# The heads-of-16 run: an order for each engine, z transposed and output weights whole in plain fp32, the norm's constant on Pool

## The chip, the cores and the metric

The kernel runs on one core of one Trainium2 chip. The metric is the device time of one execution in microseconds (us). Before the change it was 1670.71 us, the median of 3 runs (1670.12 to 1672.01). The engines are TensorE (PE in the profile, with its weight loads apart as PEld), VectorE (DVE), ScalarE (ACT), GpSimd (POOL) and SyncE (SP), which issues the DMAs.

## The reference

Two decoder layers with a norm after each part, on x of 16 sequences x 128 positions x 256 features. The six parts, each as x = norm(x + part(x)):

1. causal self-attention with 16 heads of 64
2. eight dense experts with relu (256 to 512 and back), weighted by gates that are gathered from the context
3. a gated FFN with 2 shared and 16 routed experts, top 2
4. self-attention with 16 heads of 16, only keys within 8 positions
5. cross-attention with 16 heads of 16, keys and values from ctx (16 x 128 x 128), with biases
6. eight experts with gelu (256 to 512 and back), all summed, scaled by a gate

Parts 4 and 5 are the heads-of-16 run. For part 4 the reference computes

```python
qkv = (x @ Wqkv).reshape(b, n, 3, H, HD)
attn = where(band, q @ k.T * HD ** -0.5, -1e9); attn = softmax(attn)
out = (attn @ v).transpose(0, 2, 1, 3).reshape(b, n, c) @ Wproj + bproj
x = (r - mean(r)) / sqrt(var(r) + 1e-5)      # r = x + out
```

Part 5 is the same with q from x, k and v from the context, and a bias on each.

## The kernel before, in words

**Precision.** Most products are split: an operand is held as a high part of type fp32r and a low part, the rest of it (fp32r too), and `split3` (L81 to L85) multiplies high x high, high x low and low x high into one sum. To split a tile costs two instructions: ACT writes the high part out of PSUM, DVE subtracts it from PSUM's value to get the low part. Products of plain fp32 tiles also occur (P times V, transposes by the identity); a plain fp32 product shows as two records in the trace, a transpose as one.

**Tiling of the run.** The 16 sequences go in groups of 4; the four groups of part 4 and then the four of part 5 make 8 groups G. A sequence has 16 heads in 4 quads of 4 heads, so there are 128 quads n and 32 sequences B. Step n of the run stands for quad n in all engines' programs. Per quad:

- "s": PE computes the scores of 4 heads, 128 x 512, into one of two PSUM banks (L1576 adds the band mask, L1579 the products); DVE takes the negated row maximum (L1803); ACT takes four exponentials (L1705).
- "t": PE transposes the four P tiles (L1589); DVE (even quads, L1808) or ACT (odd, L1679) copies them out.
- "pv": PE multiplies with V (L1603), the four heads in four column strips, the row sums in a 17th column.

Per sequence:

- "ze": ACT empties the bank of P-V products (L1722), the next sequence's first P-V product waits for that.
- "zb": PE transposes back (L1617). "zn" (DVE): reciprocal (L1765) and product (L1767) give z.
- "zt": PE transposes z (L1625); ACT writes its high part `nzT_h` (L1726); DVE its low part `nzT_l` (L1813).
- "o": PE's output product, 2 x split3 = 6 products of 256 columns (L83 to L85 with `nzT`), with the output weights in halves.
- "na": DVE adds the residual (L1774). "ns": DVE takes statistics (L1779, L1780) and adds the epsilon (L1781), POOL raises to the power -0.5 (L1509). "nb": DVE writes the new X (L1786).

Fills "x", "k", "q", "v" prepare the next group: transposes of X and its split, projections to K, Q and V; x two fills of 4 transposes, k and q two each, v four. They and "zb" share two PSUM banks in turn. SP then lays keys and queries out, split in halves and by head, by 24 DMAs of 128 KB a group (L1433).

**What sets the order.** Semaphores alone hold the engines together; each engine works off a list in program order. `n_order` writes the list for PE, ACT and POOL; a step n holds s(n), t(n-2), pv(n-3), then per sequence ze at lag 6 (B = (n-6)/4), zb 7, zt 8, o 9, na 9, ns 10, nb 11, then a fill of the next group and, at the end of the run, work of the next stage: "mx" (transposes of X) and "mu" (the first up products of part 6). On ACT, t of an odd quad comes ahead of s. `n_order_vector` writes DVE's list: s(n), what was put off from the step before (zn of lag 7, zt of lag 8, a fill), t(n-2), na and ns of lag 10, nb of lag 12. So an engine that meets an item whose semaphore is not there yet stands, and all behind it stands too. POOL also splits weights (`beside`): those of part 5 at quad 0, two units of part 6 at quad 16, both at once.

## Time and profile before

| | |
|---|---|
| median of 3 runs | 1670.71 us |
| the profiled execution | 1671.6 us |
| its span, first to last instruction | 1669.8 us |
| PE busy | 1544.2 us, 92% |
| PE weight loads busy | 1331.2 us, 80% |
| DVE busy | 1010.4 us, 61% |
| ACT busy | 693.9 us, 42% |
| POOL busy | 180.0 us, 11% |
| mean granted TensorE clock | 0.982 of 2.4 GHz |

The prediction is made against the profiled execution. A row of the grouped views gives an engine's instructions of one kind, how often, their busy time and mean, and the engine's idle time just before them with what ended it. A matmul's end is modelled and includes the pipeline's latency: consecutive matmuls overlap in the rows, and what one takes up of the array is the distance of the starts.

### The profile page before, as it was taken

The page shows a single profiled execution, that of the slowest core. Times are in us where ns is not written, and L with a number is a line of the kernel's source. Part 1 is how long each engine was busy: PE and PEld are TensorE (multiplying, and loading weights), DVE is VectorE, ACT ScalarE, POOL GpSimd, SP SyncE. Part 2 cuts the span into 40 slices and gives each one's busy share as a digit, 9 for nine tenths or more (in the row PEclk, how much of TensorE's full clock was granted, in tenths as well). Part 3 has the DMA queues.
Part 4 walks back from the last instruction along what each step waited for, and adds up shares of the span by engine and source line. Part 5 has one row for each costly group of instructions (what it writes and reads, how often), then busy time and mean ns, then how long its engine had stood idle before and what let it go on. Part 6 is the DMA issues. An engine that isn't in the chain of part 4 may idle for free.

```text
span 1669.8 us, 28828 instructions
## 1 busy us (share of the span) xinstructions
PE 1544.2 (92%) x11176; PEld 1331.2 (80%) x11176; DVE 1010.4 (61%) x2177; ACT 693.9 (42%) x1809; POOL 180.0 (11%) x174
## 2 busy tenths in 40 slices
PE   6999999899999999899999788887778899999997
PEld 5888888689899989888888566666557798989896
DVE  6777677755545445766656666677774554444446
ACT  1444444522222222123333566677773344444443
POOL 1222222310000000020000330111110000000001
PEclk9999999999999999989999999999997899999999
DMA  6000100011101101000001965667640000000001
GB/s 203 2 14 1 39 2 1 26 37 38 31 32 37 38 17 45 19 20 14 32 0 19 128 77 72 78 85 113 80 65 14 13 26 26 26 25 13 25 13 50
DMA packets 43067, 66.52 MB, mean 40 GB/s; under 512 B 4561, under 2 KB 33489, under 8 KB 42833
## 3 DMA queue, kind: packets, MB, share of 16 engines
q1 hardware_dynamic: 42960, 65.09, 19.8%
q8 instruction: 69, 1.13, 0.3%
q14 instruction: 38, 0.30, 0.1%
HBM read 36.24 MB, written 2.10 MB: 23 GB/s over the span
## 4 chain that ended last, share of the span: by engine, by line
PE 78%; DVE 15%; issue 2%; ACT 2%; DMA 1%; SPq 1%; POOL 0%; DVEq 0%; POOLq 0%; ACTq 0%
PE ps L83 22%; PE ps L84 21%; PE ps L85 21%; DVE negm L1803 4%; PE ps L366 2%; PE ps L390 2%; PE ps L377 2%; PE ps L1579 1%; DVE nPT L1808 1%; PE ps L360 1%; DVE nz L1767 1%; DVE X L901 1%; PE ps L1576 1%; PE ps L1603 1%; DVE nzT_l L1813 1%
## 5 line engine op out<-in xcount | busy, mean ns | idle before, releaser
L863 DVE TENSOR_TENSOR m6hT_l<-m6h,m6hT_h 128x512 fp32r<-128x512 f32 x128 | 88.5, 692 | 189.9 <-ACT m6hT_h L768 189.7
L770 ACT ACTIVATE m2hT_h<-ps 128x512 fp32r<-128x512 f32 x128 | 76.4, 597 | 285.9 <-PE ps L85 285.9
L865 DVE SCALAR_TENSOR_TENSOR m2hT_l<-ps,m2hT_h 128x512 fp32r<-128x512 f32 x128 | 88.5, 691 | 160.5 <-ACT m2hT_h L770 160.4
L767 ACT ACTIVATE m6h<-ps,m6b 128x512 f32<-128x512 f32 x128 | 88.0, 688 | 222.5 <-PE ps L85 207.9
L1705 ACT ACTIVATE nPr<-ps,negm 128x128 f32<-128x128 f32 x512 | 145.2, 371 | 72.0 <-DVE negm L1803 71.2
L83 PE MATMUL ps<-w_h,m6hT_h 128*128 128x256 f32 x512 | 145.9, 285 | 2.4 <-DVE X L901 1.8
L85 PE MATMUL ps<-w_h,m6hT_l 128*128 128x256 f32 x512 | 146.3, 286 | 0.0
L84 PE MATMUL ps<-w_l,m6hT_h 128*128 128x256 f32 x512 | 145.8, 285 | 0.0
L1803 DVE TENSOR_REDUCE negm<-ps 128x4 f32<-128x512 f32 x128 | 87.9, 688 | 89.0 <-PE ps L1579 88.3
L85 PE MATMUL ps<-m2w_h,m2hT_l 128*128 128x256 f32 x448 | 126.8, 283 | 0.0
L84 PE MATMUL ps<-m2w_l,m2hT_h 128*128 128x256 f32 x448 | 126.7, 283 | 0.0
L83 PE MATMUL ps<-m2w_h,m2hT_h 128*128 128x256 f32 x448 | 126.3, 282 | 0.0
L83 PE MATMUL ps<-m6XT_h,w_h 128*128 128x512 f32 x256 | 103.4, 404 | 9.0 <-DVE m6hT_l L863 9.0
L83 PEld LDWEIGHTS ps<-w_h,m6hT_h 128*128 128x128 f32 x512 | 98.7, 193 | 8.6 <-issue 2.4
L84 PE MATMUL ps<-m6XT_l,w_h 128*128 128x512 f32 x256 | 102.9, 402 | 0.0
L84 PEld LDWEIGHTS ps<-w_l,m6hT_h 128*128 128x128 f32 x512 | 98.7, 193 | 5.2
L85 PE MATMUL ps<-m6XT_h,w_l 128*128 128x512 f32 x256 | 102.1, 399 | 0.0
L85 PEld LDWEIGHTS ps<-w_h,m6hT_l 128*128 128x128 f32 x512 | 98.4, 192 | 0.0
L445 ACT ACTIVATE wPr<-ps,negm 128x128 f32<-128x128 f32 x256 | 90.8, 383 | 4.8 <-DVE negm L513 4.8
L83 PEld LDWEIGHTS ps<-m2w_h,m2hT_h 128*128 128x128 f32 x448 | 85.6, 191 | 4.7
L83 PE MATMUL ps<-m2XT_h,m2w_h 128*128 128x512 f32 x224 | 88.9, 397 | 0.3 <-DVE m2hT_l L865 0.2
L84 PEld LDWEIGHTS ps<-m2w_l,m2hT_h 128*128 128x128 f32 x448 | 85.6, 191 | 4.0
(288 smaller groups left out, 4274.6 us busy)
## 6 DMA issues: line engine op xcount, KB each, us to landing
nKm<-nKc_h SPq DMA_DIRECT2D x64, 128.0 KB, 4.6
nQs<-nQc_h SPq DMA_DIRECT2D x64, 128.0 KB, 6.0
raw<-in_w_e1i SPq DMA_DIRECT2D x9, 512.0 KB, 3.3
raw<-in_w_e1o SPq DMA_DIRECT2D x9, 512.0 KB, 3.3
raw<-in_w_e6i SPq DMA_DIRECT2D x9, 512.0 KB, 3.4
raw<-in_w_e6o SPq DMA_DIRECT2D x9, 512.0 KB, 3.4
raw<-in_w_a SPq DMA_DIRECT2D x8, 512.0 KB, 4.5
nKm<-nKc_l SPq DMA_DIRECT2D x32, 128.0 KB, 5.4
```

What stands on the lines that cost most here:

```text
L83: nc.tensor.matmul(out, wh, xh, start=start, stop=False, **kw)
L84: nc.tensor.matmul(out, wh, xl, start=False, stop=False, **kw)
L85: return nc.tensor.matmul(out, wl, xh, start=False, stop=stop, **kw)
L366: last = nc.tensor.matmul(ps[:, WSB[half], i * S:(i + 1) * S], W.QT[G % 2][rows64, 4 * u + i, tok], W.KT[G % 2][rows64, 4 * u + i, tok], s ...
L377: last = nc.tensor.transpose(ps[:, WTB[half], i * S:(i + 1) * S], W.Pr[:, p % 3, half, i, :], ident[:, :])
L445: last = nc.scalar.activation(W.Pr[:, p % 3, half, j, :], ps[:, WSB[half], j * S:(j + 1) * S], ACT.Exp, bias=negm[:, n % 4, j:j + 1], accu ...
L767: nc.scalar.activation(c.h32[:, u % 2, :], ps[:, u % 2, :], ACT.Gelu, bias=bias)
L770: nc.scalar.activation(c.hT[0][:, ch, :], ps[:, u % 2, :], ACT.Relu).then_inc(c.s["hi_ready"], 1)
L863: last = nc.vector.tensor_tensor(c.hT[1][:, ch, :], c.h32[:, u % 2, :], c.hT[0][:, ch, :].bitcast(F32), ALU.subtract)
L865: last = nc.vector.scalar_tensor_tensor(c.hT[1][:, ch, :], ps[:, u % 2, :], 0.0, c.hT[0][:, ch, :].bitcast(F32), ALU.max, ALU.subtract)
L1705: last = nc.scalar.activation(N.Pr[:, i % 4, j, :], ps[:, SB[i % 2], j * S:(j + 1) * S], ACT.Exp, bias=negm[:, i % 4, j:j + 1])
L1803: nc.vector.reduce_max(negm[:, i % 4, :], ps[:, SB[i % 2], :].rearrange("p (h k) -> p h k", h=QH), AX.X, negate=True).then_inc(s["s_max"], 1)
```

## The change

- Each engine gets an order of its own: `n_order` for PE, `n_order_scalar`, `n_order_vector`, `n_order_pool`. Lags before and after: PE zb 7 and 7, zt 8 and 9 (now between the scores and the P transposes), o 9 and 10; ACT ze 6 and 5, zt 8 and 8, with the copy of P of an odd quad ahead of the exponentials in both; DVE zn 8 in effect and 8, na 10 and 11, ns 10 and 14, nb 12 and 16; POOL's power 10 and 14, with the residual (na) at 11.
- Fills stand at steps 0, 2, 4, 5, 6, 8, 9, 10, 12, 14 of a group, not at 0, 1, 4 to 11. "mx" 4 and 5 stand at 13 and 14, not 11 and 12. The run has 17 steps after the last quad, not 12.
- z transposed is one plain fp32 tile `nzT` in two buffers, written by ACT alone; the low half and DVE's subtraction go. The output weights are also kept whole in fp32 (`wo4`, `wo5`, in the room of their low halves), and the output product is 2 plain fp32 products of 256 columns, not 6 split ones.
- `split_unit` writes the whole copy with `tensor_copy`, in place of the subtraction.
- The addition of the norm's epsilon moves from DVE to POOL, which then waits for itself before the power.
- POOL's splits are single units at quads 3, 7, 19 and 23.

```diff
-    A5.wq, A5.wk, A5.wv, A5.wo = view(wA5, 0, DC, D), view(wA5, 512, 1, D), view(wA5, 768, 1, D), view(wA5, 1024, DC, D)
+
+    wo4 = Region(nc, r3.start + (2048 + 1536) * 4, 2 * KB).place("wo4", [P, DC * D], F32)
+    wo5 = Region(nc, r1.start + (1536 + 1024) * 4, 2 * KB).place("wo5", [P, DC * D], F32)
+    A4.wo, A5.wo = (w[:, :].rearrange("p (k n) -> p k n", k=DC) for w in (wo4, wo5))
+    A5.wq, A5.wk, A5.wv = view(wA5, 0, DC, D), view(wA5, 512, 1, D), view(wA5, 768, 1, D)
...
-    def split_unit(v, base, k, w, ncols, on=nc.vector, quarter=None):
+    def split_unit(v, base, k, w, ncols, on=nc.vector, quarter=None, whole=None):
+
...
         on.tensor_scalar(w[0], raw[k % 2][:, 0:ncols], 1.0, None, ALU.mult).then_inc(split_hi, 1)
         v.wait_ge(split_hi, base + (k + 1))
+        if whole is not None:
+            n_whole = whole.shape[1]
+            last = on.tensor_copy(whole, raw[k % 2][:, ncols - n_whole:ncols])
+            if n_whole < ncols:
+                last.then_inc(split_whole, 1)
+                on.tensor_tensor(w[1][:, 0:ncols - n_whole], raw[k % 2][:, 0:ncols - n_whole], w[0][:, 0:ncols - n_whole].bitcast(F32),
+                                 ALU.subtract).then_inc(split_whole, 1)
+                v.wait_ge(split_whole, 2)
+                v.sem_inc(prep_done, 1)
+            else:
+                last.then_inc(prep_done, 1)
+            return
         on.tensor_tensor(w[1], raw[k % 2][:, 0:ncols], w[0].bitcast(F32), ALU.subtract).then_inc(prep_done, 1)
...
-    N.zT = pair(m, "nzT", [P, DC, S])
+    N.zT = m.place("nzT", [P, 2, DC, S], F32)
...
-    M_X_AT = (6, 7, 8, 9, 11, 12)
+    M_X_AT = (6, 7, 8, 9, 13, 14)
...
-        return [("x", (G, 0)), ("x", (G, 1)), None, None, ("k", (G, 0)), ("k", (G, 1)), ("q", (G, 0)), ("q", (G, 1)),
-                ("v", (G, 0)), ("v", (G, 1)), ("v", (G, 2)), ("v", (G, 3))]
+        at = {0: ("x", 0), 2: ("x", 1), 4: ("k", 0), 5: ("k", 1), 6: ("q", 0), 8: ("q", 1),
+              9: ("v", 0), 10: ("v", 1), 12: ("v", 2), 14: ("v", 3)}
+        return {k: (kind, (G, j)) for k, (kind, j) in at.items()}
+    def n_fill_of(n):
+        G, k = divmod(n, NQ)
+        return [n_fills(G + 1)[k]] if G + 1 < NGG and k in n_fills(G + 1) else []
+    def n_quad(kind, n, lag=0):
+        return [(kind, n - lag)] if 0 <= n - lag < NQUADS else []
+    def n_seq(kind, n, lag):
+        return [(kind, (n - lag) // 4)] if (n - lag) % 4 == 0 and 0 <= (n - lag) // 4 < NSEQS else []
+    N_STEPS = NQUADS + 17
     def n_order():
-        order = [f for f in n_fills(0) if f]
-        for n in range(NQUADS + 12):
-            G, k = divmod(n, NQ)
-            step = [("s", n), ("t", n - 2), ("pv", n - 3)]
-            step += [(kind, (n - at) // 4) for kind, at in (("ze", 6), ("zb", 7), ("zt", 8), ("o", 9), ("na", 9), ("ns", 10), ("nb", 11))
-                     if (n - at) % 4 == 0]
-            of = {"s": NQUADS, "t": NQUADS, "pv": NQUADS}
-            order += [(kind, i) for kind, i in step if 0 <= i < of.get(kind, NSEQS)]
-            if G + 1 < NGG and k < 12 and n_fills(G + 1)[k]:
-                order.append(n_fills(G + 1)[k])
-            order += n_following(n)
+        order = list(n_fills(0).values())
+        for n in range(N_STEPS):
+            order += n_quad("s", n) + n_seq("zt", n, 9) + n_quad("t", n, 2) + n_quad("pv", n, 3)
+            order += n_seq("zb", n, 7) + n_seq("o", n, 10) + n_fill_of(n) + n_following(n)
+        return order
+    def n_order_scalar():
+        order = list(n_fills(0).values())
+        for n in range(N_STEPS):
+            order += n_quad("t", n, 2) + n_quad("s", n) + n_seq("ze", n, 5) + n_seq("zt", n, 8) + n_fill_of(n) + n_following(n)
+        return order
+    def n_order_vector():
+        order = list(n_fills(0).values())
+        for n in range(N_STEPS):
+            order += n_quad("s", n) + n_seq("zn", n, 8) + n_quad("t", n, 2)
+            order += n_seq("nb", n, 16) + n_seq("ns", n, 14) + n_seq("na", n, 11)
+            order += n_fill_of(n - 1) + n_following(n - 1)
+        return order
+    def n_order_pool():
+        order = []
+        for n in range(N_STEPS):
+            order += n_quad("s", n) + n_seq("na", n, 11) + n_seq("ns", n, 14)
         return order
     def n_following(n):
-    def n_order_vector():
-        order = [f for f in n_fills(0) if f]
-        late = []
-        for n in range(NQUADS + 13):
-            G, k = divmod(n, NQ)
-            steps = [("s", n)] if n < NQUADS else []
-            steps += late
-            if 0 <= n - 2 < NQUADS:
-                steps.append(("t", n - 2))
-            steps += [(kind, (n - at) // 4) for kind, at in (("na", 10), ("ns", 10), ("nb", 12))
-                      if (n - at) % 4 == 0 and 0 <= (n - at) // 4 < NSEQS]
-            late = [(kind, (n - at) // 4) for kind, at in (("zn", 7), ("zt", 8))
-                    if (n - at) % 4 == 0 and 0 <= (n - at) // 4 < NSEQS]
-            if G + 1 < NGG and k < 12 and n_fills(G + 1)[k]:
-                late.append(n_fills(G + 1)[k])
-            late += n_following(n)
-            order += steps
-        return order
...
-        for kind, i in n_order():
+        for kind, i in n_order_pool():
             if kind == "ns":
                 b = i % GB
                 pool.wait_ge(s["ln_var"], i + 1)
+                nc.gpsimd.tensor_scalar(veps[:, b:b + 1], mv[:, b, 1:2], LN_EPS, None, ALU.add).then_inc(s["eps_added"], 1)
+                pool.wait_ge(s["eps_added"], i + 1)
                 nc.gpsimd.tensor_tensor(rstd[:, b:b + 1], veps[:, b:b + 1], mhalf[:, b:b + 1],
                                         ALU.pow).then_inc(s["rstd_ready"], 1)
             elif kind == "na" and i % GB == GB - 1 and i + 1 < NSEQS:
                 residual(i // GB + 1)
+            elif kind == "s" and i in beside:
+                beside[i]()
             elif kind == "s" and i % NQ == 0:
                 G = i // NQ
-                if G in beside:
-                    beside[G]()
                 if NG - 1 <= G < NGG - 1:
                     context(G - NG + 1)
 
...
-                last = split3(nc, ps[:, EB, D:2 * D], N.zT[0][:, ch, :], N.zT[1][:, ch, :],
-                              c.wo[0][:, ch, :], c.wo[1][:, ch, :], ch == 0, ch == DC - 1)
+                last = nc.tensor.matmul(ps[:, EB, D:2 * D], N.zT[:, B % 2, ch, :], c.wo[:, ch, :],
+                                        start=ch == 0, stop=ch == DC - 1)
...
-        for kind, i in n_order():
+        for kind, i in n_order_scalar():
...
-                if i >= NQUADS - 2 and i % 2:
+                if i % 2:
                     transposed_p(i)
             elif kind == "s":
-                if i >= 2 and i % 2:
-                    transposed_p(i - 2)
                 act.wait_ge(s["s_max"], i + 1)
...
-                nc.scalar.activation(N.zT[0][:, :, :].rearrange("p a b -> p (a b)"), ps[:, EB, 0:D],
-                                     ACT.Identity).then_inc(s["zt_hi"], 1)
+                nc.scalar.activation(N.zT[:, i % 2, :, :].rearrange("p a b -> p (a b)"), ps[:, EB, 0:D],
+                                     ACT.Identity).then_inc(s["zt_ready"], 1)
...
-            link(nc.vector.bn_aggr(mv[:, b, :], stats[:, b, :]))
-            nc.vector.tensor_scalar(veps[:, b:b + 1], mv[:, b, 1:2], LN_EPS, None, ALU.add).then_inc(s["ln_var"], 1)
+            nc.vector.bn_aggr(mv[:, b, :], stats[:, b, :]).then_inc(s["ln_var"], 1)
...
-            elif kind == "zt":
-                v.wait_ge(s["zt_hi"], i + 1)
-                nc.vector.tensor_tensor(N.zT[1][:, :, :].rearrange("p a b -> p (a b)"), ps[:, EB, 0:D],
-                                        N.zT[0][:, :, :].rearrange("p a b -> p (a b)").bitcast(F32),
-                                        ALU.subtract).then_inc(s["zt_ready"], 1)
...
-            def split_a5():
-                for k in range(2):
-                    split_unit(pool, U_A5, k, cut(wA5, k * 768, 768), 768, nc.gpsimd, quarter=(2 * D, 3) if k == 0 else None)
-            def split_e6():
-                for k in range(2):
-                    split_unit(pool, U_E6, k, cut(slots6[0], k * RAW, RAW), RAW, nc.gpsimd)
-            n_pool(pool, {0: split_a5, 1: split_e6})
+            def split_a5(k):
+                split_unit(pool, U_A5, k, cut(wA5, k * 768, 768), 768, nc.gpsimd, quarter=(2 * D, 3) if k == 0 else None,
+                           whole=None if k == 0 else wo5[:, :])
+            def split_e6(k):
+                split_unit(pool, U_E6, k, cut(slots6[0], k * RAW, RAW), RAW, nc.gpsimd)
+            n_pool(pool, {3: lambda: split_a5(0), 7: lambda: split_a5(1), 19: lambda: split_e6(0), 23: lambda: split_e6(1)})
             mix_pool(pool, M6)
 
```

## Rows read from the trace of the kernel before

**Rows 1.** The page's busy table: engine, busy us, share of span, instructions.
```profile
PE 1544.2 (92%) x11176; PEld 1331.2 (80%) x11176; DVE 1010.4 (61%) x2177; ACT 693.9 (42%) x1809; POOL 180.0 (11%) x174
```

**Rows 2.** The row maxima by line: count, shortest/median/longest ns, first and last start.
```profile
L1803 DVE TENSOR_REDUCE negm<-ps x128: 680/691/693, 928.1 to 1255.2; 128x4 f32<-128x512 f32 x128
```

**Rows 3.** Windows: stretch, length, busy PE, PEld, DVE, ACT, POOL, clock, DMA, GB/s.
```profile
967.30:1012.00 44.70, 38.36 (x346) 28.79 (x345) 29.60 (x67) 29.07 (x87) 13.97 (x9) 1.00 0.58 72
...
1099.10:1139.40 40.30, 32.28 (x313) 24.35 (x312) 29.73 (x67) 29.61 (x88) 6.36 (x8) 1.00 0.65 87
...
1220.00:1255.20 35.20, 27.38 (x286) 20.14 (x288) 27.61 (x62) 27.79 (x85) 3.96 (x4) 1.00 0.46 69
```

**Rows 4.** Waits, 928 to 1268 us: us in total, times, longest.
```profile
ACT nPr L1705 <- DVE negm L1803: 71.2, 77, 11.9
...
PE ps L1625 <- DVE nz L1767: 19.6, 31, 0.9
...
PE ps L83 <- DVE nzT_l L1813: 13.2, 30, 0.7
PE ps L1603 <- issue: 9.2, 14, 0.8
...
PE ps L1603 <- ACT nzr L1722: 5.5, 7, 0.8
```

**Rows 5.** Waits of PE's weight loads, 928 to 1268 us.
```profile
PEld ps L1625 <- DVE nz L1767: 28.8, 32, 1.3
PEld ps L83 <- DVE nzT_l L1813: 21.6, 30, 1.0
...
PEld ps L1617 <- issue: 6.5, 31, 0.2
```

**Rows 6.** Lines by form, 960 to 1260 us: count, busy, mean ns, idle before.
```profile
L1576 PE MATMUL ps<-band,identb 128*128 128x512 bf16 x51 | 19.7, 387 | 0.0
...
L1509 POOL TENSOR_TENSOR rstd<-veps,mhalf 128x1 f32<-128x1 f32 x29 | 16.0, 550 | 190.2 <-DVE veps L1781 190.2
...
L1813 DVE TENSOR_TENSOR nzT_l<-ps,nzT_h 128x256 fp32r<-128x256 f32 x30 | 12.5, 415 | 0.0
```

**Rows 7.** Timeline, 1060 to 1082 us: start, length, instruction, merged count.
```profile
1059.82 0.41 PE L1603 MATMUL ps<-nPT,nV 128*17 128x128 f32 x8
...
1060.42 1.14 ACT L1705 ACTIVATE nPr<-ps,negm 128x128 f32<-128x128 f32 x4
...
1060.79 0.28 PE L84 MATMUL ps<-wA_l,nzT_h 128*128 128x256 f32 x1
...
1061.27 0.28 PE L85 MATMUL ps<-wA_h,nzT_l 128*128 128x256 f32 x1
```

**Rows 8.** Plain fp32 products of part 1 (by tile, then timeline) and bf16.
```profile
L390 PE MATMUL ps<-wPT,wV x416: 272/273/324, 62.9 to 299.6; 128*64 128x128 f32 x139
...
150.22 1.09 PE L390 MATMUL ps<-wPT,wV 128*64 128x128 f32 x16
...
151.25 0.60 PE L360 MATMUL ps<-causal,identb 128*128 128x512 bf16 x2
```

**Rows 9.** SP's issue of a layout DMA; the page's issues with landing.
```profile
1166.00 0.61 SPq L1433 DMA_DIRECT2D nQs<-nQc_h  x1
...
nQs<-nQc_h SPq DMA_DIRECT2D x64, 128.0 KB, 6.0
```

**Rows 10.** Timeline, the run's last sequence.
```profile
1267.13 0.38 ACT L1726 ACTIVATE nzT_h<-ps 128x256 fp32r<-128x256 f32 x1
...
1268.44 1.23 DVE L640 TENSOR_TENSOR w_l<-raw,w_h 128x1024 fp32r<-128x1024 f32 x1
...
1270.38 0.58 PE L83 MATMUL ps<-wA_h,nzT_h 128*128 128x256 f32 x1 [3.29 <-DVE nzT_l L1813]
```

**Rows 11.** Windows at the same place.
```profile
1265.40:1268.80 3.40, 0.81 (x4) 0.20 (x2) 2.82 (x6) 1.65 (x3) 0.39 (x1) 1.00 0.00 0
1268.80:1272.20 3.40, 1.82 (x8) 1.82 (x9) 1.66 (x4) 0.00 (x0) 0.00 (x0) 0.50 0.38 105
```

More of the change, by code:

```diff
@@ L170, in program @@
     split_hi = sem("split_hi")
+    split_whole = sem("split_whole")
     raw_loaded = [sem("raw_loaded0"), sem("raw_loaded1")]
@@ L195, in program @@
     A4.wq, A4.wk, A4.wv = ([t[:, :, i * D:(i + 1) * D] for t in qkv4] for i in range(3))
-    A4.wo = view(wA4, 1536, DC, D)
-    A5.wq, A5.wk, A5.wv, A5.wo = view(wA5, 0, DC, D), view(wA5, 512, 1, D), view(wA5, 768, 1, D), view(wA5, 1024, DC, D)
+    wo4 = Region(nc, r3.start + (2048 + 1536) * 4, 2 * KB).place("wo4", [P, DC * D], F32)
+    wo5 = Region(nc, r1.start + (1536 + 1024) * 4, 2 * KB).place("wo5", [P, DC * D], F32)
+    A4.wo, A5.wo = (w[:, :].rearrange("p (k n) -> p k n", k=DC) for w in (wo4, wo5))
+    A5.wq, A5.wk, A5.wv = view(wA5, 0, DC, D), view(wA5, 512, 1, D), view(wA5, 768, 1, D)
     A4.mask, A4.cross, A4.bq, A4.bk, A4.bv, A4.bo = band, False, None, None, None, row_bo4
@@ L1296, in steps @@
                         n, at = (768, k * 768) if k < 2 else (256, 1536 + (k - 2) * 256)
-                        split_unit(v, U_A4, k, cut(wA4, at, n), n, quarter=(D, k + 1) if k < 2 else None)
+                        split_unit(v, U_A4, k, cut(wA4, at, n), n, quarter=(D, k + 1) if k < 2 else None, whole=None if k < 2 else wo4[:, (k - 2) * D:(k - 1) * D])
                 elif kind == "c":
@@ L1349, in program @@
     N.s = signals("n", "g_full g_evac xt_hi qk_hi ct_hi ct_ready ctx_loaded s_full s_max p_ready pt_full pt_even pt_odd z_full "
-                       "z_zeroed zr_ready zb_full rec_done z_ready zt_full zt_hi zt_ready o_full r_done xb_ready ln_var rstd_ready x_done")
+                       "z_zeroed zr_ready zb_full rec_done z_ready zt_full zt_ready eps_added o_full r_done xb_ready ln_var rstd_ready x_done")
     N.q_laid = [sem(f"n_q_laid{j}") for j in range(2)]
```

## Prediction, before the changed kernel ran

> **What bounds the kernel now.** I read the page's busy table first [rows 1]: TensorE (PE) is busy 92% of the span. A share over all stages says little here, since the edit touches one stage, the heads-of-16 run, whose row maxima run from 928.1 to 1255.2 us, 128 of them, one per quad of heads [rows 2]. So I listed where those maxima start and cut the stage there, at every 16th, which is a group of 4 sequences [rows 3]. A group takes 44.7 us in the banded attention, 40.3 us in the cross attention, and 35.2 us at the end, where no projections of a next group lie in between. PE is busy 38.4, 32.3 and 27.4 us of these; VectorE (DVE) 29.6, 29.7, 27.6; ScalarE (ACT) 29.1, 29.6, 27.8. The granted clock is 1.00 (2.4 GHz). No engine is full: PE leads, and stands still at fixed places once per sequence.
>
> The waits name these places. PE's matmuls wait 19.6 us in 31 waits for z (the transposes of z, L1625), 13.2 us in 30 waits for the low half of z transposed (the output product's first, L83), and 9.2 + 5.5 us in 14 + 7 waits ahead of the P-V products (L1603), whose bank ACT has still to empty [rows 4]. The matmul rows understate it, because a matmul's modelled end reaches past the time in which it takes up the array. PE's weight loads show the hole itself: 28.8 us in 32 waits and 21.6 us in 30, against 0.21 us (6.5 in 31) that even a wait released in time leaves [rows 5].
>
> **Part by part, per sequence (32 of them).**
>
> 1. z's transposes go from the step that follows the division (lags 8 and 7 quads in PE's and DVE's order) to lag 9, behind that step's scores. The hole of 0.90 us shrinks to the usual 0.21: 0.69.
> 2. The output product goes from lag 9 to 10 and no longer waits for DVE. Today PE transposes z, ACT writes the high half (0.38 us [rows 10]), DVE, in its next step behind the maximum, the low half (0.415) [rows 6], and PE stands before it. Now ACT alone writes zT and PE has more than a step of other work. 0.72 less 0.21: 0.51.
> 3. The evacuation of z (kind "ze") moves up on ACT from lag 6 to 5, so it lies ahead of the exponentials of step 4B+6, and the P-V products at step 4B+7 find their bank free: 14.7/32 = 0.46.
> 4. Against it: the product itself. The split products start 0.12 us apart (four intervals from 1060.79 to 1061.27 [rows 7]): 0.72 for the six. Two plain fp32 products replace them. The trace has no plain fp32 product of 256 columns. It has 128-column ones [rows 8]: each is two records; 16 records in two concurrent column halves take 1.09 us, the last of them 0.27, so 0.82 for 7 intervals, 0.77 without the slow first (0.324 against 0.273): 0.11 for a pass over 128 columns. Two bf16 products of 512 columns take 0.60 together, the last of them 0.39 [rows 6, 8], so 0.21 to 0.22 for 512 columns: the plain pass is twice as slow per column. That product loads 64 columns of weights; L1603 with 17 loaded columns starts its second round after about the same 0.13 (0.41 less 0.28 [rows 7]), so it is not the load. At that rate: 2 products x 2 passes x 2 x 0.11 = 0.88 us, 0.16 more than today. The lower bound, if 0.11 were the time of any pass however long: 4 x 0.11 = 0.44, or 0.28 less than today. I take 0.88: the nearest row is the same kind of product; with the cheap end the sum below would be 14 us lower.
>
> The Trainium skill (FP8 and Floating Point Precision, section TensorE Precision Notes) says that true FP32 makes four passes through the array. By it two products of 256 columns would take 4 × 256 / 2.4 × 2 = 0.85 us, an estimate; it speaks against this edit as a saving on PE and sides with my dearer end.
>
> Sum per sequence: 0.69 + 0.51 + 0.46 − 0.16 = 1.50 us closable, 48.0 us for 32.
>
> 5. How much of it comes through? With all of it a cross-attention sequence would take 10.07 − 1.50 = 8.6 us. ACT needs 29.6/4 = 7.4 of that, its work unchanged in amount: 86%. DVE loses the low half (0.415) [rows 6] and a 128x1 addition: under 7.0, or 81%. 86% is just the share that PE holds in the banded groups today (38.4 of 44.7), the highest of any engine in this stage. So the full sum lies at the edge; and ACT now waits in its order for two things that PE issues a step later. I take two thirds, 1.0 us, and 32.0 us for the stage. Bounds: one third (16 us) and the whole with the cheap product (62 us).
> 6. DVE's relief and the spread of its work over the four steps of a sequence are not on the path: it is busy 29.7 of 40.3 us. Worth nothing by itself; without it, item 5 would be tighter.
> 7. Pool gets the epsilon add: a 128x1 operation beside a power of 0.55 us on the same shape [rows 6], between 0.1 and 0.6 us plus a semaphore round. DVE's "nb" asks for it 2 quads (over 4 us) after "ns"; Pool stands idle 190 us in this stretch before those powers. Nothing. If that cover went it would cost 0.6 per sequence on DVE, not on PE. Behind it on Pool stand the residual of the next group and the context split, both asked for more than a step later.
> 8. Weight preparation: the output weights keep their high pass and get a copy in place of the subtraction (two DVE units, equal instruction count), and Pool issues one instruction more, of 512 columns, at the start of the stage for weights used in its second half. Splitting the next stage's weights as two single units at steps 19 and 23 instead of both at 16 leaves Pool's powers less blocked; none of the large waits [rows 4] is for Pool, so nothing.
> 9. The fills stand further apart, q's second at step 8 instead of 7. SP lays out the queries behind it: 6 issues of 0.61 us and 6.0 us to landing [rows 9], some 10 us, with 7 steps (over 15 us) to go. SP's second half (12 issues and a landing, 13.3 us) must be there by step 8, 17 us at the new pace. The last two transposes of X for the next stage move from steps 11 and 12 to 13 and 14, behind the norm that they need (step 12 for sequence 27). Nothing.
> 10. The drain. For the last sequence PE stands 3.29 us before the output product, since DVE's low half waits behind the split of the next stage's weights, whose second instruction alone takes 1.23 us [rows 10]. ACT's copy of zT ends at 1267.51; with nothing of DVE between, the product could start by 1267.8 instead of 1270.38: 2.5 us. What follows on the chain to the last X (statistics, Pool, norm) gets up to 0.6 longer by Pool's add and lies beside the first down products and one up product. In the same stretch the granted clock falls to 0.50 (1.2 GHz) after PE had been busy 0.81 of 3.4 us, and PE works 1.82 of the next 3.4 us at it [rows 11], and, busy throughout, 3.4 us more; without the fall these 5.2 us would take 2.6 less. Between 0 and 2.6; I take 0, since nothing says that the fall would not then come at the next gap.
>
> Sum: 32.0 + 2.5 = 34.5 us. The profiled execution took 1671.6 us (span 1669.8 and 1.8 around it): 1637.1. It stands 0.9 above the median 1670.71, so against the median 1636.
>
> **Rivals.**
>
> A, all holes close: items 1 to 4 in full, the drain and the clock: 48.0 + 2.5 + 2.6 = 53.1, 1618 us. For it: ACT waits 71.2 us for the maximum alone [rows 4], more than it would have to give. Against: 86% on ACT in order.
>
> B, ACT or DVE become the bound early: a third of the holes comes through, 16 + 2.5 less, 1652 us. For it: the group without projections, where PE has 7.8 us of slack, still takes 35.2 us with three engines at 27.4 to 27.8. So more than PE's holes paces it.
>
> C, slower: ACT's new places. "ze" at lag 5 stands ahead of the next exponentials and waits for P-V products that PE issues in its next step, behind that step's scores and P transposes and behind whatever projection the step before had; "zt" at lag 8 likewise. A projection of six 512-column products is 6 × 0.22 = 1.3 us, four P transposes and the P-V products at 0.11 a pass some 0.6 more: up to 1.9 us of standing at each, 3.8 per sequence. ACT has 10.07 − 7.4 = 2.7 us to spare. From there on it costs: 1.1 us in each of the 28 sequences beside projections, +31 us, 1702 us. It speaks against it that the exponentials ahead of "ze" last 1.14 us [rows 7] and the P copy comes on top, which covers nearly all of a step without a projection, and that two score banks let PE run ahead.
>
> D, no change: an unseen loop of scores, maximum, exponentials sets the step. The loop is about 0.5 + 0.69 + 1.14 and latencies, 2.5 us for two quads, 1.25 per quad, while a quad takes 2.2 to 2.8. Hardly.
>
> **Chances.** Forecast (1625 to 1646) 0.55; A (below 1625) 0.17; B (1646 to 1667) 0.15; within 0.2% (3.3 us, what a measurement of this kernel can tell) 0.04; C 0.09. So faster 0.87, same 0.04, slower 0.09. The range 1616 to 1660 leaves out part of B and all of C.
>
> **What would show it.** In the changed profile: groups near 40 and 36 us instead of 44.7 and 40.3; PE's weight loads ahead of z's transposes and of the output product with holes near 0.2; the "nzr" wait gone; plain products of zT as four records per sequence, about 0.22 us apart (0.11 would be rival A's cheap end); ACT's share above 80% in a group, and its waits for the scores' maximum halved from 71 us. New ACT waits of over 1 us before its copies of z or zT, or PE waiting for exponentials, would be B or C. Pool's adds under 0.6 us, nobody waiting. I am wrong if groups stay above 42 and 39 us.

## The result, and the profile after

The changed kernel takes 1615.92 us (median of 4 runs, 1614.77 to 1618.39) against 1671.03 us for the kernel before (median of 4 here): ratio 0.9672, 95% interval 0.9655 to 0.9689, 55 us faster. I had forecast 1636. The direction was right and the mechanism mostly so; the size was not: the time lies on the lowest edge of the range of 1616 to 1660, where rival A (all holes close, 1618) stood with a chance of 0.17.

The stage first. These are windows of the changed kernel, cut like [rows 3] at the first row maximum of a banded group, of a cross group, and of the last one (stretch, length, busy PE, PEld, DVE, ACT, POOL, clock, DMA share, GB/s):

```profile
965.90:1003.90 38.00, 38.00 (x339) 29.04 (x338) 30.09 (x59) 28.40 (x88) 15.90 (x13) 1.00 0.63 84
1076.70:1108.60 31.90, 31.90 (x305) 24.54 (x303) 27.63 (x58) 28.35 (x87) 7.40 (x12) 1.00 0.81 109
1172.40:1206.80 34.40, 28.90 (x273) 21.03 (x272) 24.83 (x52) 27.09 (x83) 5.47 (x9) 0.95 0.47 76
```

The banded group fell from 44.7 to 38.0 us, the cross group from 40.3 to 31.9, and in both PE's busy time fills the stretch: no hole is left that its modelled ends would show. The last group did not follow (35.2 to 34.4, and its window covers 15 quads, as that of before does); PE stands in it for 5.5 us, and its granted clock was 0.95, not 1.00, which is 1.7 us at full rate. Starts of the row maxima give the sum: the first seven groups took 291.9 us and take 241.0, 50.9 less; from the start of the last group to the end of the span 449.8 and 444.2, 5.6 less; the run starts 3.3 us later in this execution (931.4 against 928.1 us), which differs from execution to execution: f3 and e4 below, with the same code up to there, start at 927.4 and 928.6. Together 53.2, the difference of the spans (1669.8 and 1616.6).

The waits of the changed kernel over 928 to 1215 us (total, times, longest) answer to [rows 4, 5]:

```profile
DVE negm L1828 <- PE ps L1607: 44.7, 78, 1.5
ACT nPr L1731 <- DVE negm L1828: 23.3, 32, 12.3
...
ACT nzT L1752 <- PE ps L1653: 18.3, 22, 2.8
...
PEld ps L1645 <- issue: 6.5, 31, 0.2
PEld ps L1662 <- issue: 6.5, 31, 0.2
PE ps L707 <- DVE m6XT_l L866: 5.0, 4, 2.2
...
PEld ps L1653 <- DVE nz L1793: 1.1, 3, 0.4
```

PE's hole before the transposes of z is 1.1 us in all (2.4 with the run's last sequence, at 1220) where it was 28.8; the output product's weights (L1662) start after the plain 0.21. ACT now waits 18.3 us for the transposes of z, the wait that rival C feared; in the full groups it costs nothing, since PE has no hole there. ACT's waits for the maximum fell from 71.2 us to 23.3 (one wait of 11.9 and of 12.3 us in each). Of the forms in 960 to 1210 us (count, busy us, mean ns, idle before) four answer to parts of the sum:

```profile
L1731 ACT ACTIVATE nPr<-ps,negm 128x128 f32<-128x128 f32 x460 | 131.9, 383 | 9.7 <-DVE negm L1828 9.7
...
L1662 PE MATMUL ps<-wo,nzT 128*128 128x256 f32 x116 | 32.8, 405 | 0.0
...
L1811 DVE TENSOR_SCALAR X<-nr,mv,rstd 128x256 f32<-128x256 f32 x29 | 14.2, 489 | 0.0
...
L1535 POOL TENSOR_SCALAR veps<-mv 128x1 f32<-128x1 f32 x29 | 6.3, 218 | 199.3 <-DVE mv L1806 199.3
```

And one output product in the timeline, four records merged, which take 1.13 us with the last one's 0.379 in it; behind it the run's last:

```profile
1176.11 1.13 PE L1662 MATMUL ps<-wo,nzT 128*128 128x256 f32 x4
...
1220.65 1.13 PE L1662 MATMUL ps<-wo,nzT 128*128 128x256 f32 x4 [0.47 <-ACT nzT L1752]
```

1.13 − 0.38 = 0.75 for three intervals, the first of them longer by 0.1 for the start after a wait: 0.216 a pass.

### The profile page after: what moved, and what is told of

It is laid out like the page before. It is cut to its first block, busy times and chain, and to the rows that moved or that the text cites. A ratio compares the mean times of both kernels' runs of the same rounds, so it can differ in the third digit from the quotient of the medians.

```text
span 1616.6 us, 28670 instructions
## 1 busy us (share of the span) xinstructions
PE 1541.5 (95%) x11112; PEld 1330.8 (82%) x11112; DVE 998.3 (62%) x2113; ACT 687.4 (43%) x1809; POOL 187.6 (12%) x207
## 3 DMA queue, kind: packets, MB, share of 16 engines
q8 instruction: 69, 1.13, 0.3%
## 4 chain that ended last, share of the span: by engine, by line
PE 86%; DVE 8%; DMA 2%; issue 2%; ACT 2%; SPq 1%; POOL 1%; DVEq 0%; POOLq 0%; ACTq 0%
PE ps L83 22%; PE ps L84 21%; PE ps L85 21%; PE ps L1617 3%; PE ps L1631 2%; PE ps L370 2%; PE ps L394 2%; PE ps L1662 2%; PE ps L1607 2%; PE ps L381 2%; PE ps L1645 1%; DMA nQs<-nQc_h 1%; PE ps L364 1%; PE ps L1604 1%; SPq L1459 1%
## 5 line engine op out<-in xcount | busy, mean ns | idle before, releaser
L1731 ACT ACTIVATE nPr<-ps,negm 128x128 f32<-128x128 f32 x512 | 146.7, 383 | 23.3 <-DVE negm L1828 23.3
L83 PE MATMUL ps<-w_h,m6hT_h 128*128 128x256 f32 x512 | 145.3, 284 | 2.4 <-DVE X L918 1.8
L83 PE MATMUL ps<-m2w_h,m2hT_h 128*128 128x256 f32 x448 | 126.3, 282 | 0.0
L1828 DVE TENSOR_REDUCE negm<-ps 128x4 f32<-128x512 f32 x128 | 88.2, 689 | 45.5 <-PE ps L1607 44.7
L83 PE MATMUL ps<-m6XT_h,w_h 128*128 128x512 f32 x256 | 103.6, 405 | 8.8 <-DVE m6hT_l L880 8.8
L83 PEld LDWEIGHTS ps<-w_h,m6hT_h 128*128 128x128 f32 x512 | 97.9, 191 | 8.6 <-issue 2.4
L817 POOL TENSOR_TENSOR rstd<-veps,mhalf 128x4 f32<-128x4 f32 x8 | 9.2, 1150 | 701.6 <-DVE veps L933 701.6
L83 PEld LDWEIGHTS ps<-m2w_h,m2hT_h 128*128 128x128 f32 x448 | 85.6, 191 | 4.7
L83 PE MATMUL ps<-m2XT_h,m2w_h 128*128 128x512 f32 x224 | 88.9, 397 | 0.3 <-DVE m2hT_l L882 0.2
```

Source lines behind the costliest of these rows:

```text
L83: nc.tensor.matmul(out, wh, xh, start=start, stop=False, **kw)
L1731: last = nc.scalar.activation(N.Pr[:, i % 4, j, :], ps[:, SB[i % 2], j * S:(j + 1) * S], ACT.Exp, bias=negm[:, i % 4, j:j + 1])
L1828: nc.vector.reduce_max(negm[:, i % 4, :], ps[:, SB[i % 2], :].rearrange("p (h k) -> p h k", h=QH), AX.X, negate=True).then_inc(s["s_max"], 1)
```

## The experiments

All ratios are against the kernel before, run in the same job, whose median lay between 1670.2 and 1671.9 us. "Changed" is the changed kernel. Differences in us are those of the medians; where the ratios give another figure, both stand.

**Orders without the arithmetic (e1).** On the changed kernel:

```diff
-    N.zT = m.place("nzT", [P, 2, DC, S], F32)
+    N.zT = pair(m, "nzT", [P, DC, S])
...
-                last = nc.tensor.matmul(ps[:, EB, D:2 * D], N.zT[:, B % 2, ch, :], c.wo[:, ch, :], ...)
+                last = split3(nc, ps[:, EB, D:2 * D], N.zT[0][:, ch, :], N.zT[1][:, ch, :],
+                              c.wo[0][:, ch, :], c.wo[1][:, ch, :], ch == 0, ch == DC - 1)
...
-            order += n_quad("s", n) + n_seq("zn", n, 8) + n_quad("t", n, 2)
+            order += n_quad("s", n) + n_seq("zn", n, 8) + n_seq("zt", n, 9) + n_quad("t", n, 2)
```

> The changed kernel's four orders, fills and Pool's places, but the arithmetic of before: z transposed and the output weights in halves, six split products, the low half taken by DVE at lag 9, the epsilon added by DVE. Theory (the orders close the holes, the arithmetic does not matter for them; the two plain products hold the array 4 x 0.216 = 0.86 us against 0.70 for the six split ones): PE is now the bound, so this is about 32 x 0.16 = 5 us faster than the changed kernel, 1611 us. Rival (the arithmetic is what closed the hole before the output product, by taking DVE out of it): the hole before L83 with nzT comes back at 0.5 us, 32 x 0.5 = 16 us, so 1627 us or more.

Measured 1619.06 us, ratio 0.9691 (0.9671 to 0.9710). The orders alone bring 51 of the 55 us; the interval overlaps that of the changed kernel, so on top of them the arithmetic's worth is not resolved. Its windows (two groups and the last):

```profile
963.00:1000.40 37.40, 37.40 (x347) 28.90 (x346) 31.94 (x67) 28.40 (x87) 14.91 (x9) 1.00 0.62 86
1072.10:1103.40 31.30, 31.30 (x313) 24.41 (x312) 29.13 (x67) 28.41 (x87) 6.40 (x8) 1.00 0.84 112
1165.90:1201.00 35.10, 29.03 (x280) 21.55 (x279) 26.30 (x59) 26.85 (x83) 4.55 (x5) 0.90 0.47 74
```

Half of the theory holds: six split products are cheaper for PE than two plain ones, 0.6 us a group from the second on, or 0.15 a sequence (I had said 0.16); the first group is 0.8 us longer. The other half fails: from the last group's start to the end this kernel takes 1617.6 − 1165.9 = 451.7 us, the changed one 444.2. For the last sequence DVE's low half stands behind the weights' split again, as in [rows 10], and PE's weight loads wait for it:

```profile
PEld ps L83 <- DVE nzT_l L1835: 3.4, 1, 3.4
```

The clock differs too. In the three windows of 50 us from the start of the last group it was 0.93, 0.74 and 0.95 in e1, 0.97, 0.80 and 1.00 in the changed kernel: 7.5 us of full rate more lost in e1, as much as the whole difference. The wait and the clock are not told apart here; PE ran at 1.2 GHz right behind the wait (its next records start 0.21 us apart instead of 0.12), but no run varies one without the other.

**The arithmetic without the orders (e2).** The kernel before with the plain product, ACT's single copy, the whole weights and the epsilon on Pool; the diff is the changed kernel's own for these.

> The kernel before with the changed arithmetic alone (zT whole by ACT, two plain products, whole output weights, epsilon on Pool), the orders of before. Theory (orders make the gain): of the closed holes only that before the output product goes (13 to 16 us), less 5 us for dearer products, plus the 2.5 us at the drain: about 1671 - 11 = 1660 us. Rival (arithmetic makes it): a third to a half of the 55 us, 1645 us or less. Third: it is slower than before, 1676 us, if the ACT copy stands behind other ACT work and the hole stays.

Measured 1653.33 us, ratio 0.9902 (0.9880 to 0.9923): 17 us, more than the 11 of the theory, less than the rival's 26. A banded group takes 43.1 us and a cross group 38.1, by the starts of the maxima. The hole before the output product is gone, that before the transposes of z stays. The rest lies beyond my terms: the waits before the projections shrank by 2.7 us (table under "How the parts add"), and in the profiled execution 3 us less of full rate was lost from the last group on. Waits over 967 to 1200 us:

```profile
PEld ps L1642 <- DVE nz L1784: 20.8, 23, 0.9
...
PEld ps L1651 <- issue: 4.8, 23, 0.2
```

**The z lags alone (g4).** The kernel before, PE's list with zt at 9 behind the scores and o at 10; residual, statistics and norm a step later:

```diff
-            step = [("s", n), ("t", n - 2), ("pv", n - 3)]
+            step = [("s", n)] + (of_seq(("zt", 9)) if pe else []) + [("t", n - 2), ("pv", n - 3)]
...
+            step += of_seq(("ze", 6), ("zb", 7), *([] if pe else [("zt", 8)]), ("o", 10), ("na", 10), ("ns", 11), ("nb", 12))
...
-            steps += [... for kind, at in (("na", 10), ("ns", 10), ("nb", 12)) ...]
+            steps += [... for kind, at in (("na", 11), ("ns", 11), ("nb", 13)) ...]
```

> The kernel before with PE's transposes of z at lag 9 behind the scores and the output product at lag 10; residual, statistics and norm follow one step later. Arithmetic, fills and all else as before. Theory (these two lags are the largest part; taking them out of the changed kernel cost 21 us and closes 0.69 + 0.5 us of holes for 32 sequences here): 1671 less 21 to 38 us, 1633 to 1650 us. Rival (DVE's low half now stands ahead of its copy of P and waits for PE and ACT in the same step, so the hole moves to the P-V products): over 1660 us.

Measured 1632.98 us, ratio 0.9772 (0.9751 to 0.9794): 38 us from two lags, 1.18 a sequence, where items 1 and 2 of the prediction add to 1.20. Windows of a banded and a cross group, and the P-V products' wait for the bank:

```profile
1006.00:1045.20 39.20, 38.13 (x347) 28.91 (x346) 29.82 (x68) 28.68 (x87) 4.54 (x5) 1.00 0.69 82
1081.60:1115.80 34.20, 31.94 (x311) 24.34 (x310) 29.68 (x68) 28.68 (x87) 6.39 (x7) 1.00 0.78 102
```
```profile
PE ps L1603 <- ACT nzr L1722: 3.7, 4, 2.1
PE ps L1603 <- issue: 1.7, 4, 0.7
```

ze stands at lag 6 here as before, and yet the 5.5 + 9.2 us before L1603 have shrunk to 3.7 + 1.7: most of that hole followed from the others.

**The z lags taken back (f4).** The changed kernel, with PE's zt at lag 8 behind the P-V products and o at 9:

```diff
-            order += n_quad("s", n) + n_seq("zt", n, 9) + n_quad("t", n, 2) + n_quad("pv", n, 3)
-            order += n_seq("zb", n, 7) + n_seq("o", n, 10) + n_fill_of(n) + n_following(n)
+            order += n_quad("s", n) + n_quad("t", n, 2) + n_quad("pv", n, 3)
+            order += n_seq("zb", n, 7) + n_seq("zt", n, 8) + n_seq("o", n, 9) + n_fill_of(n) + n_following(n)
```

> The changed kernel with PE's order alone as before for z's transposes (lag 8, behind the P-V products) and the output product (lag 9). Theory: PE stands again for z, 0.6 us for 32 sequences, but not for the output product, since ACT alone writes z transposed: 19 us, 1635 us. Rival: the hole does not come back because DVE's division now stands ahead of its copy of P: under 5 us.

Measured 1636.82 us, ratio 0.9786 (0.9757 to 0.9816): 21 us lost, 19 by the ratios, the theory's figure. As expected the hole for z returns and no other (967 to 1180 us):

```profile
PEld ps L1653 <- DVE nz L1793: 22.3, 23, 1.3
```

**The fills, added and taken back (g3, f2).** In the kernel before, fills at steps 0, 2, 4, 5, 6, 8, 9, 10, 12, 14; in the changed kernel, at 0, 1, 4 to 11 (f2's edit is shown):

```diff
-        at = {0: ("x", 0), 2: ("x", 1), 4: ("k", 0), 5: ("k", 1), 6: ("q", 0), 8: ("q", 1),
-              9: ("v", 0), 10: ("v", 1), 12: ("v", 2), 14: ("v", 3)}
+        at = {0: ("x", 0), 1: ("x", 1), 4: ("k", 0), 5: ("k", 1), 6: ("q", 0), 7: ("q", 1),
+              8: ("v", 0), 9: ("v", 1), 10: ("v", 2), 11: ("v", 3)}
```

> The kernel before with one edit: the fills at steps 0, 2, 4, 5, 6, 8, 9, 10, 12, 14. Theory (additive: taking the spread out of the changed kernel cost 15 us): 1656 us. Rival (the steps are set by the holes for z, the fills only matter once those are closed): over 1665 us.

> The changed kernel with the fills of the next group at steps 0, 1, 4 to 11 as before. Theory (in the profile of before PE also stood in the fills, so spreading them is worth something that the prediction left out): groups that now take 37.9 and 31.9 us become 1 to 2 us longer, 7 groups, 1623 to 1630 us. Rival (fills are covered by any order without the holes): within 3 us of 1616.

Added: 1654.87 us, ratio 0.9897 (0.9872 to 0.9921), 16 us, 17 by the ratios. Taken back: 1631.44 us, ratio 0.9745 (0.9716 to 0.9774), 15 us lost, 12 by the ratios. The two agree within that; the prediction had put the fills at nothing. With the fills together PE stands before the projections, waiting for one of the two banks that fills and "zb" share: DVE's division of z (`nz`) has still to read zb's, or DVE's copy of a projection the other. The kernel f2 over 967 to 1180 us, and behind it all that the changed kernel has at L83 in the same stretch:

```profile
PEld ps L83 <- issue: 10.9, 27, 1.0
PE ps L83 <- DVE nz L1793: 4.3, 6, 0.7
PEld ps L83 <- DVE nQc_l L1773: 2.8, 4, 0.7
```
```profile
PEld ps L83 <- issue: 6.3, 30, 0.2
```

**ze back at lag 6 (f1).**

```diff
-            order += n_quad("t", n, 2) + n_quad("s", n) + n_seq("ze", n, 5) + n_seq("zt", n, 8) + ...
+            order += n_quad("t", n, 2) + n_quad("s", n) + n_seq("ze", n, 6) + n_seq("zt", n, 8) + ...
```

> The changed kernel with ACT's emptying of the P-V bank (ze) back at lag 6, all else changed. Theory (each of three moved items closes a hole of its own): the hole before the P-V products of every fourth quad returns, 0.46 us for each of 32 sequences, 15 us: 1631 us. Rival (ACT and PE now have slack there, the other moves give it away): within 3 us of 1616.

Measured 1615.08 us, ratio 0.9651 (0.9629 to 0.9673): nothing lost (0.8 us below the changed kernel, 3.5 by the ratios, within overlapping intervals). The rival holds.

**DVE's order back (g2).**

```diff
-            order += n_quad("s", n) + n_seq("zn", n, 8) + n_quad("t", n, 2)
-            order += n_seq("nb", n, 16) + n_seq("ns", n, 14) + n_seq("na", n, 11)
-            order += n_fill_of(n - 1) + n_following(n - 1)
+            order += n_quad("s", n) + n_seq("zn", n, 8) + n_fill_of(n - 1) + n_following(n - 1) + n_quad("t", n, 2)
+            order += n_seq("na", n, 11) + n_seq("ns", n, 11) + n_seq("nb", n, 13)
```

> The changed kernel with DVE's order as before: fills ahead of the copy of P, residual, statistics and norm close together (lags 11, 11, 13, Pool's power at 11). Theory (what is left of the gain after the z lags, 21 us, the fills, 15 us, and the arithmetic, 3 us, comes from DVE's work spread over the steps): 1625 to 1632 us. Rival (DVE has slack, its order is worth nothing; the parts overlap instead): within 3 us of 1616.

Measured 1619.60 us, ratio 0.9692 (0.9675 to 0.9710), 3 or 4 us, with intervals that still overlap. In the trace the banded groups are unchanged (37.9 us), the cross groups 33.2 instead of 31.9. The theory's 9 to 16 us are two and a half to four times too large.

**The epsilon on DVE again (e3).** `bn_aggr` is followed by DVE's `tensor_scalar(veps, ...)` as before, Pool only raises to the power.

> The changed kernel with the norm's epsilon added by DVE again. Theory (off the path, PE is the bound): within 2 us of 1616. Rival (Pool's small operations cost DVE and its norm, whose mean rose from 406 to 489 ns in the profile): the norm's mean falls back towards 410 ns, and the kernel is faster by up to 3 us; or, if DVE was the bound, 5 us slower.

Measured 1616.57 us, ratio 0.9670 (0.9653 to 0.9688): nothing. The norm's mean hardly falls (489 to 472 ns), so it does not come from the small additions. The changed kernel's, listed by tile (shortest/median/longest ns):

```profile
L1811 DVE TENSOR_SCALAR X<-nr,mv,rstd x29: 402/404/2195, 967.7 to 1209.5; 128x256 f32<-128x256 f32 x29
```

Two of the 29 make the mean: one of 2.20 us at 975.68 and one of 1.09 us at 987.10. Each begins while POOL subtracts for the split of part 6's weights (`w_l<-raw,w_h`, 2.38 us from 975.34 and from 985.65); DVE's copy of P, which reads PSUM, kept its 680 ns beside the same two. e3 has the same pair (1.94 and 0.83 us); in the kernel before no norm of the run took over 0.41 us. The two long norms go with that split, then, and not with the additions.

**The last group (e4, f3, g1).** In the changed kernel's last group ACT must not overwrite the queries' tile before the layout DMA has landed, and PE's transposes of X for the next stage share one bank, so that each waits for DVE to empty it (1172 to 1207 us):

```profile
PE ps L707 <- DVE m6XT_l L866: 5.0, 4, 2.2
...
ACT m6XT_h L792 <- DMA nQs<-nQc_h: 1.6, 1, 1.6
```

e4 moves the six transposes later:

```diff
-    M_X_AT = (6, 7, 8, 9, 13, 14)
+    M_X_AT = (9, 10, 11, 12, 13, 14)
```

> The changed kernel with the six transposes of X for the next stage at steps 9 to 14 of the last group, not at 6 to 9, 13, 14. Theory (in the last group ACT stands 4 us at step 6 before it may overwrite the queries' tile, until the layout DMA of that group's second half has landed, and what follows is late): the last group falls from 34.4 us (15 intervals) to 28 to 30, the kernel to 1610 or 1612 us. Rival (the second half's scores at step 8 need the same DMA, so the stall only moves from ACT to PE): 1 us or nothing.

1615.60 us, ratio 0.9674 (0.9658 to 0.9691): nothing; the last group takes 35.6 us at a granted clock of 0.90, steps 10 to 14 now 2.7 to 4.4 each, and PE's wait at L707 is still 4.1 us. The stall at the DMA was not the price. f3 instead puts DVE's low half ahead in its step:

```diff
+            mx = n_following(n - 1)[:1] if n <= NQUADS else []
-            order += n_quad("s", n) + n_seq("zn", n, 8) + n_quad("t", n, 2)
+            order += n_quad("s", n) + mx + n_seq("zn", n, 8) + n_quad("t", n, 2)
...
-            order += n_fill_of(n - 1) + n_following(n - 1)
+            order += n_fill_of(n - 1) + (n_following(n - 1) if not mx else [])
```

> The changed kernel with one move in DVE's order: in the last group the low half of X transposed for the next stage comes right behind the step's row maximum, not at the end of the step. Theory (the six transposes share one bank, PE's next one waits for DVE's subtraction of the last, 1.6 and 2.2 us in the profile): the waits of L707 fall from 5.0 us to under 2, the last group from 34.4 to about 31, 1612 us, or 1610 if a fall of the clock goes too. Rival (the wait for the layout DMA alone delays the last group): 1616.

1613.11 us, ratio 0.9649 (0.9625 to 0.9674): 3 us below the changed kernel, 4 by the ratios, with intervals that overlap. The last group takes 33.0 us, not 31, and of the 1.4 us gained there the clock alone (1.00 instead of 0.95) can be all; PE's wait at L707 fell only to

```profile
PE ps L707 <- DVE m6XT_l L866: 3.8, 4, 1.3
```

g1 joins e1's arithmetic to f3 and moves the next stage's weight split behind the last norm (`order += [("mw", M_EARLY - 1)] if n == NQUADS + 12 else []`).

> The changed orders with the split output product (as in e1), DVE's low half of X for the next stage right behind the maximum (as in f3), and the split of the next stage's weights moved from ahead of the last sequence's low half to behind its norm. Theory (PE bound in seven groups: six split products are 0.14 us a sequence shorter, e1's groups were 0.5 to 0.6 us shorter each; e1 lost that again at the seam, where the low half stood behind the weights' split): 4 us below f3, about 1609 us. Rival (the low half costs PE at the drain all the same): 1613 to 1617 us.

1613.74 us, ratio 0.9657 (0.9643 to 0.9672), not 1609, and 0.6 us above f3. The groups from the second to the seventh are 0.5 to 0.6 us shorter as in e1. But from the last group's start to the end the profiled execution takes 1615.0 − 1166.9 = 448.1 us, f3's 442.7. In that stretch the clock stood otherwise; two of the windows, g1 first:

```profile
1216.70:1220.10 3.40, 3.40 (x18) 3.40 (x18) 2.40 (x7) 0.00 (x0) 1.09 (x2) 0.50 0.00 0
...
1226.90:1237.20 10.30, 10.30 (x44) 9.72 (x45) 1.26 (x2) 1.26 (x2) 0.00 (x0) 0.50 0.01 2
```
```profile
1216.70:1220.10 3.40, 3.40 (x26) 3.14 (x25) 2.24 (x7) 0.00 (x0) 0.88 (x3) 1.00 0.46 146
...
1226.90:1237.20 10.30, 10.30 (x59) 9.72 (x59) 2.52 (x3) 1.27 (x2) 0.00 (x0) 0.67 0.13 39
```

Here g1 loses 1.7 + 1.75 us more of full rate. From 1237.2 to 1257.7 us it is the other way (0.92 against 0.84, 1.6 us back), in the last group and from 1257.7 to 1400 us again g1's loss (0.95 against 1.00, and 0.96 against 0.98). Over the whole stretch g1 loses 5 to 6 us more of full rate, as much as the 5.4 us between the times. These are single executions, and g1's is the slowest of its five (1617.22 us, the others 1612.19 to 1614.20); what made the clock fall was not tested. So g1 says nothing against the 0.15 us a sequence, nor can it show that they reach the end.

## Why the prediction was right or wrong

**Right.** PE's holes were the bound, and the places were the named ones: the table below shows the waits at them closed. Items 1 and 2 (0.69 + 0.51 a sequence, 38 us) are what g4 measured alone, 38 us. In the table below g4's waits for z and before the output product fall by 20.5 + 13.5 = 34.0 us in 28 sequences, 1.21 each. That the totals meet to the microsecond is in part luck: 6 us before the P-V products closed too, and other waits rose. Item 4 was sized right: 0.22 us a pass expected, 0.216 measured, and the dearer end applied; the edit is a cost on PE of 0.15 a sequence, which e1's shorter groups show. The Trainium skill's four passes for true FP32 (FP8 and Floating Point Precision, TensorE Precision Notes) agree: an estimate of 0.85 us for the two products by it, and in the trace four records, 4 × 0.216 = 0.86 us. Items 6 and 7 hold within a few us (g2, e3). Item 10: PE's 3.29 us before the last output product became 0.47 (the run's last output product above), so the 2.5 taken were sound. The stretch from the last group on fell by 5.6 us, most of it through the clock, which the item priced at 0 to 2.6 and took at 0: in the three windows of 50 us from the last group's start it was 0.99, 0.74 and 0.97 before, 0.97, 0.80 and 1.00 after, 3.5 us less lost.

**Wrong, the step that failed: item 5.** I let two thirds of the closable time through, since 86% was the highest share any engine had reached. It came through whole, and more: 50.9 us in 28 sequences, 1.82 each, against 1.0 taken and 1.50 as the most. 86% was PE's share because PE stood in holes, not a ceiling. With them closed PE fills the groups; in the cross groups DVE reaches 87% (93% in e1) and ACT 89% beside it, while both still wait. That the time still meets the edge of the range is luck: no term of the range stood for the fills, the next point.

**Wrong, left out: item 9's fills.** Their spread is worth 12 to 17 us (f2, g3), about half a microsecond a sequence. The view behind [rows 4] had shown part of it in small entries, the projections waiting for a bank, which I did not add up; item 9 looked only at the layout DMAs:

```profile
PE ps L83 <- DVE nQc_l L1747: 2.6, 4, 0.7
PE ps L83 <- DVE nV L1759: 2.2, 4, 0.6
PE ps L83 <- DVE nV L1757: 1.6, 3, 0.5
```

They add to 6.4 us. The rest of the fills' worth was in the hole before the P-V products (table below, g3).

**Wrong, a cause misread: item 3.** ze at lag 5 is worth nothing (f1), and its hole closed in part in g4 and in part in g3, both with ze at lag 6. A wait that "ACT nzr" ends was here a consequence of steps drawn out elsewhere. The hole did close in the changed kernel, so the 0.46 in the sum was right as a size and wrong as a cause.

**How the parts add.** Alone on the kernel before: z lags 38, arithmetic 17, fills 16, together 71 us, where the change brings 55. Taken from the changed kernel: z lags 21, fills 15, DVE's order 3 to 4, arithmetic 3 (not resolved), ze and epsilon 0. The traces show where the two sums part. The table adds up, over the first seven groups (from the run's first maximum to that of the last group), the waits of PE's weight loads by what they were for, in us:

| kernel | seven groups | all waits | P-V | z | output | projections |
|---|---|---|---|---|---|---|
| before | 291.9 | 102.2 | 31.6 | 23.6 | 19.0 | 13.6 |
| z lags alone (g4) | 256.0 | 65.3 | 25.6 | 3.1 | 5.5 | 13.8 |
| fills alone (g3) | 273.0 | 81.6 | 24.3 | 24.5 | 15.9 | 4.8 |
| arithmetic alone (e2) | 279.5 | 85.3 | 31.5 | 23.5 | 5.5 | 10.9 |
| fills taken back (f2) | 255.7 | 62.0 | 18.3 | 2.3 | 5.5 | 18.6 |
| z lags taken back (f4) | 260.3 | 67.3 | 18.3 | 25.1 | 5.5 | 4.8 |
| changed | 241.0 | 46.6 | 18.3 | 0.0 | 5.5 | 7.6 |

Each group time follows the waits within 2 us, once the dearer product (0.16 × 28 = 4.5 us) is added where it stands. The three edits alone take 35.9 + 18.9 + 12.4 = 67.2 us off the seven groups, together 50.9. The difference, 16.3, is about the hole before the output product, counted more than once: z lags and arithmetic each close its 13.5 us, and the fills 3.1 of them.

**Rival C** did not occur: ACT's wait for the transposes of z exists (18.3 us) but lies in ACT's spare time. Rival B's evidence, the group without projections, was misleading. PE stood in it at the same places as elsewhere (1220 to 1255.2 us of the kernel before):

```profile
PEld ps L1603 <- issue: 5.8, 16, 1.0
PEld ps L1625 <- DVE nz L1767: 3.6, 4, 0.9
PEld ps L83 <- DVE nzT_l L1813: 2.6, 4, 0.7
PEld ps L690 <- DVE m6XT_l L849: 1.1, 2, 0.6
```

With the z lags alone (g4) the group falls to 31.6 us. In the changed kernel it stays at 34.4, with new waits in the place of the old: PE's own before the transposes for the next stage rose from 0.9 to 5.0 us (L707), and the clock was 0.95.

**What stays open.** The last group (34.4 us for 15 quads with PE busy 28.9) and the clock's falls in it and behind it, which differ from run to run by more than the last experiments were to resolve. No version tried is below the changed kernel beyond the intervals; f3 and g1 are the lowest by median, f3 and f1 by ratio.

## What to carry to other kernels

In an in-order pipeline, when the fullest engine stands at fixed places, move what it waits for by a step before making anything shorter: two lags brought 38 us here, and the busy share seen with the holes is no ceiling for the share without them. Add up an engine's small waits too, above all those for shared banks. Where PE was full, the edit that spares DVE at PE's cost, a gain of 17 us before, was a loss of 0.15 us a sequence. And edits that close the same hole do not add: list the waits by place before adding up the parts.

## What the runs showed that I had not expected

ACT's exponentials take 383 ns on average in the changed kernel and in e3, 371 in the kernel before, with equal shape. It comes with the z lags: over 960 to 1200 us the mean is 381 in g4, which moves only them, and 371 and 370 in g3 and e2. Those that ACT starts after a wait take 367 or 368 in both kernels; no run says more of the cause. The layout DMAs' share of the DMA engines' time rose to 0.81 to 0.84 in the cross groups without anybody waiting for them but at the last group.
